# Inverse softmax sums and layer 3 outputs turned by 32x32 blocks on the vector engine and moved by DMA, in a four-layer graph network kernel

## The reference

```python
# layer 0
scores = einsum('bhid,bhjd->bhij', q, k) / sqrt(HD) + edge_bias
attn = softmax(where(adj_mask, scores, -inf), axis=-1)
out = einsum('bhij,bhjd->bhid', attn, v) ...   # then @ W_o.T
# layer 3
e = leaky_relu(e_i[:, :, :, None] + e_j[:, :, None, :], 0.2)
attn = softmax(where(adj > 0, e, -9e15), axis=-1)
out = einsum('bhnm,bhmd->bhnd', attn, h) ...
```

## Time and profile before

| | |
|---|---|
| median of 3 runs | 1429.56 us |
| profiled execution | 1432.08 us, of it the span from first to last instruction 1430.3 us |
| PE busy | 1352.1 us, 95% |
| DVE busy | 1191.3 us, 83% |
| ACT busy | 1188.4 us, 83% |
| POOL busy | 663.1 us, 46% |
| DMA queue of SP | 23618 packets, 44.27 MB, 9.8% of 16 engines' span |
| mean granted TensorE clock | 0.976 |

### The profile page before, as it was taken

One profiled execution on the slowest core, in us unless ns is written; L12 is line 12 of the kernel. 1 busy time (PEld: TensorE's weight loads), 2 busy tenths in 40 slices (PEclk: granted clock), 3 DMA queues, 4 the chain that ended last, 5 costly groups with the idle time before them and its releaser, 6 DMA issues.

```text
span 1430.3 us, 40514 instructions
## 1 busy us (share of the span) xinstructions
PE 1352.1 (95%) x13178; PEld 1075.1 (75%) x13267; DVE 1191.3 (83%) x3407; ACT 1188.4 (83%) x4353; POOL 663.1 (46%) x1014
## 2 busy tenths in 40 slices
PE   4799999999999999999999999999999999999964
PEld 3577788877778887777888777788877778887642
DVE  6568888888888888888888888888888888886763
ACT  3867888889888888998888899888889988887654
POOL 1133445554444555444455544445554444555532
PEclk7899999999999999999999999999999999999986
DMA  3100110011111001111100111111011111100000
GB/s 117 38 31 31 31 31 17 16 39 38 39 38 39 25 16 39 38 38 39 39 29 12 39 39 38 38 39 34 6 39 39 38 39 38 33 8 16 9 15 23
DMA packets 23825, 46.86 MB, mean 33 GB/s; under 512 B 2753, under 2 KB 2754, under 8 KB 23490
## 3 DMA queue, kind: packets, MB, share of 16 engines
q1 hardware_dynamic: 23618, 44.27, 9.8%
HBM read 35.88 MB, written 8.39 MB: 31 GB/s over the span
## 4 chain that ended last, share of the span: by engine, by line
PE 78%; DVE 10%; POOL 5%; issue 4%; ACT 3%; DVEq 0%; POOLq 0%; ACTq 0%
PE B L591 18%; PE B L689 14%; PE B L499 12%; PE B L537 5%; PE B L558 4%; DVE B L1353 4%; DVE x L1326 3%; POOL rstd L376 3%; PE B L808 2%; PE B L523 2%; PE B L788 2%; PE B L754 2%; PE B L581 2%; PE B L665 2%; PE B L683 2%
## 5 line engine op out<-in xcount | busy, mean ns | idle before, releaser
L995 ACT ACTIVATE e<-B,nm 128x128 f32<-128x128 f32 x1024 | 363.9, 385 | 12.5 <-DVE nm L1361 12.0
L499 PEld LDWEIGHTS B<-ident,e 128*128 128x128 f32 x1536 | 187.0, 144 | 104.3 <-issue 75.7
L499 PE MATMUL B<-ident,e 128*128 128x128 f32 x1536 | 230.0, 281 | 9.2 <-ACT e L1151 3.9
L995 ACT ACTIVATION_READ_ACCUMULATOR e<-B,nm 128x1 f32 x1024 | 231.9, 226 | 0.0
L1353 DVE SCALAR_TENSOR_TENSOR B<-an,rowb,mask 128x512 f32<-128x512 f32 x256 | 194.2, 794 | 19.0 <-ACT pT L1004 9.5
L1151 ACT ACTIVATE e<-l,nm 128x128 f32<-128x128 f32 x512 | 198.9, 400 | 10.0 <-DVE nm L1582 9.9
L1361 DVE TENSOR_REDUCE nm<-B 128x4 f32<-128x512 f32 x256 | 166.5, 683 | 35.0 <-PE B L537 34.8
L1004 ACT ACTIVATE pT<-B 128x512 f32<-128x512 f32 x256 | 157.9, 617 | 44.5 <-PE B L499 41.3
L373 POOL TENSOR_TENSOR veps<-meanv,eps 128x4 f32<-128x4 f32 x128 | 41.8, 326 | 328.9 <-DVE meanv L1320 328.8
L376 POOL TENSOR_TENSOR rstd<-veps,neghalf 128x4 f32<-128x4 f32 x128 | 139.7, 1092 | 10.0
L1582 DVE TENSOR_REDUCE nm<-l 128x4 f32<-128x512 f32 x128 | 87.0, 679 | 41.9 <-ACT l L1141 41.9
(11 more groups left out here) (201 smaller groups left out, 3471.1 us busy)
## 6 DMA issues: line engine op xcount, KB each, us to landing
xt<-in_x_t SPq DMA_DIRECT2D x32, 256.0 KB, 3.1
an<-in_adj_n SPq DMA_DIRECT2D x32, 256.0 KB, 2.7
xn<-in_x_n SPq DMA_DIRECT2D x32, 256.0 KB, 3.3
at<-in_adj_t SPq DMA_DIRECT2D x32, 256.0 KB, 3.2
out_x<-xo SPq DMA_DIRECT2D x32, 256.0 KB, 3.5
wm<-in_mats SPq DMA_DIRECT2D x1, 1088.0 KB, 9.4
wm<-in_mats SPq DMA_DIRECT2D x1, 832.0 KB, 7.1
wm<-in_mats SPq DMA_DIRECT2D x1, 320.0 KB, 3.0
```

The costliest lines, as they stand in the source:

```text
L499: last = mm(g(dst, b), g(src, b), ident[:, :], is_transpose=True, start=(b == 0), stop=True, skip_group_check=True)
L995: last = fn(g(e0[:, h % 2, :], b), g(bank, b), ACT.Exp, bias=nm0[:, h % 4, b:b + 1], accum_out=sum0[s % 2][:, b, head(h):head(h) + 1])
```

## The change

Two round trips leave PE and ACT, and the schedule lists of all engines are written anew.

- `spread_sums`, `sums_T` and `keep_sums` are gone. `invert_sums` writes the reciprocals with heads outside. A new `turn_sums` (DVE) transposes the 128 x 32 reciprocals by 32x32 blocks into `recb`. SP writes `recb` to a buffer in HBM with four DMAs of 4 KB (rows of 128 bytes) and reads it back into `recT` with one DMA that repeats each row on 16 partitions.
- `keep_out3` and `out3_T` are gone. A new `turn_out3` (DVE) transposes the 128 x 512 bank by 32x32 blocks into `o3b`. SP writes `o3b` to HBM with one DMA of 256 KB and reads it back into `o3n` with four DMAs of 64 KB, each for 32 partitions, in pieces of 128 bytes, which puts the blocks where a full transpose has them. `divide3` reads `o3n`.
- The five lists are reordered; the banks and the tuples of last users go with them. The program has 41 steps instead of 48.

```diff
-STEPS = GROUPS + 16
+MOVED = 4 * DMA
+STEPS = GROUPS + 9
+            def write_blocks(s, done, sent, got, here, there):
+                wait(sp, q[got], MOVED * s)
+                sp.wait_ge(q[done], s + 1)
+                sp.dma_start(there[:, :], here[:, :]).then_inc(q[sent], DMA)
+            def read_blocks(s, sent, got, there, here):
+                sp.wait_ge(q[sent], DMA * (s + 1))
+                for c in range(4):
+                    sp.dma_start(here[32 * c:32 * c + 32, :].rearrange("r (b i j) -> r b i j", b=GB, i=4),
+                                 there.rearrange("(i r) (b c j) -> c r b i j", i=4, b=GB, c=4)[c]).then_inc(q[got], DMA)
+            def write_sums(s):
+                wait(sp, q["recT_got"], DMA * s)
+                sp.wait_ge(q["rbt_done"], s + 1)
+                for i in range(4):
+                    sp.dma_start(inv_mem.rearrange("h (b i j) -> i (h b) j", b=GB, i=4)[i],
+                                 recb[32 * i:32 * i + 32, :]).then_inc(q["rb_sent"], DMA)
+            def read_sums(s):
+                wait(sp, q["oT_ready"], s)
+                sp.wait_ge(q["rb_sent"], MOVED * (s + 1))
+                sp.dma_start(recT[:, :], inv_mem.unsqueeze(1).broadcast_to([H0, D0, GB * N])).then_inc(q["recT_got"], DMA)
             def step(t):
+                store(t - 8)
                 load_xt(t)
+                write_out3(t - 6)
+                read_out3(t - 6)
+                load_xn(t - 1)
                 load_an(t)
-                load_xn(t)
-                store(t - 8)
                 load_at(t - 1)
+                write_sums(t - 1)
+                read_sums(t - 1)
...
+            def turn_sums(s):
+                wait(dve, q["rb_sent"], MOVED * s)
+                dve.wait_ge(q["rec_done"], s + 1)
+                v.transpose(recb[:, :], rec0[:, :, :].rearrange("p h b -> p (h b)")).then_inc(q["rbt_done"], 1)
...
+            def turn_out3(s, bank):
+                wait(dve, q["o3_sent"], DMA * s)
+                dve.wait_ge(q["pv3_ps"], s + 1)
+                v.transpose(o3b[:, :], bank[:, :]).then_inc(q["o3b_done"], 1)
...
```

More of the change, by code:

```diff
@@ L561, in values @@
                 last.then_inc(q["pv_ps"], 1)
[L563 to L571, removed]
             def project_out(s, bank, users):
@@ L1004, in keep_probs @@
                 fn(pT0[:, h, :], bank[:, :], ACT.Copy).then_inc(q["pT_ready"], 1)
-            def keep_sums(s, bank):
-                if not live(s):
-                    return
-                wait(act, q["oT_ready"], s)
-                act.wait_ge(q["recT_ps"], s + 1)
-                fn(recT[:, :], bank[:, :], ACT.Copy).then_inc(q["recT_ready"], 1)
             def keep_x1(s, bank):
@@ L1655, in step @@
-                norm0(t - 11)
-                half_tanh(t - 12)
-                stats2(t - 13)
-                row_max(t - 10, 7, B[7])
-                aggr2(t - 13)
-                divide3(t - 15, B[4])
-                edge_mask(t - 9)
-                residual3(t - 15)
-                seed_edges(t - 9, 0, B[5], (("pT3_ready", -5, 4, 2), ("pT_ready", -1, 8, 5),
-                    ("exp_done", -1, 8, 5), ("m1_done", -3, 1, 1), ("exp_done", -1, 8, 1)))
-                invert_sums(t - 10)
@@ new lines, in step @@
+                invert_sums(t - 4)
+                shared_to_all(t - 5, B[3])
+                turn_sums(t - 4)
+                message_bias(t - 5, B[4])
+                row_max(t - 3, 0, B[2])
+                row_max(t - 3, 1, B[5])
+                stats3(t - 9)
+                z_times_n(t - 6)
+                row_max(t - 3, 2, B[6])
+                gru_out(t - 6)
+                row_max(t - 3, 3, B[0])
+                sides(t - 5)
+                aggr3(t - 9)
+                shared_to_phases(t - 5, B[3])
@@ new lines, in step @@
+                turn_out3(t - 8, B[2])
+                shared_to_halves(t - 5, B[3], B[2], (("o3b_done", -3, 1, 1), ("exp_done", 2, 8, 1),
+                    ("pT3_ready", -3, 4, 2), ("tz_ready", -1, 1, 1), ("pT_ready", 1, 8, 4),
+                    ("v_ready", 1, 1, 1), ("xc_ready", -1, 1, 1)))
+                stats1(t - 6, B[1])
+                aggr1(t - 6)
+                norm3(t - 9)
+                divide(t - 4, B[7])
+                row_max3(t - 7, 0)
+                seed_edges(t - 3, 4, B[7], (("oT_ready", -1, 1, 1), ("pT_ready", -1, 8, 8),
+                    ("dd_ready", -2, 1, 1), ("qT_ready", 0, 1, 1), ("tr_ready", -3, 1, 1),
+                    ("exp_done", -1, 8, 5)))
@@ new lines, in step @@
+                seed_edges(t - 3, 5, B[5], (("l3_done", -4, 4, 1), ("exp_done", 0, 8, 2),
+                    ("g1_done", -3, 1, 1), ("exp_done", -1, 8, 6)))
+                hidden_bias(t - 6, (B[0], B[6]))
+                norm1(t - 6, B[1])
+                hidden_times_e(t - 6)
+                row_max3(t - 7, 1)
+                seed_edges(t - 3, 6, B[1], (("ln_out1", -3, 1, 1), ("pT_ready", 0, 8, 1),
+                    ("pT3_ready", -5, 4, 3), ("ej_ready", -4, 1, 1), ("pT_ready", -1, 8, 7),
+                    ("x3T_ready", -4, 1, 1), ("exp_done", -1, 8, 7)))
@@ new lines, in step @@
+                seed_edges(t - 3, 7, B[4], (("h3_ready", -4, 1, 1), ("l3_done", -4, 4, 2),
+                    ("pT_ready", 0, 8, 2), ("pT3_ready", -5, 4, 4), ("m1_done", -2, 1, 1),
+                    ("exp_done", -1, 8, 8)))
+                residual0(t - 4, B[6])
+                invert_sums3(t - 8)
+                stats0(t - 4)
+                row_max(t - 3, 4, B[7])
+                row_max(t - 3, 5, B[5])
+                aggr0(t - 4)
+                row_scales(t - 6, (B[3], B[6]))
+                residual2(t - 6, (B[3], B[6]))
@@ L1697, in _ @@
+                stats2(t - 6)
+                aggr2(t - 6)
+                row_max(t - 3, 6, B[1])
+                row_max3(t - 7, 2)
+                divide3(t - 8)
+                residual3(t - 8)
+                edge_mask3(t - 4)
+                norm0(t - 4)
+                row_max(t - 3, 7, B[4])
+                norm2(t - 6)
+                half_tanh(t - 5)
             for t in range(STEPS):
```

497 lines of the change are left out of this document (220 added, 277 removed).

## The result

The changed kernel takes 1433.07 us in the median (1430.38 to 1436.82) against 1430.01 us for the kernel before on the same chip (1428.88 to 1431.28), a ratio of 1.0023 with a 95% interval of 1.0012 to 1.0034. The forecast was 1407 us. The transposes and copies are gone, and the time did not fall.

What follows compares the result with a forecast made beforehand. PE was taken as the bound. From the profiled 1432.1 us, -27.8 for transposes, +1.5 for new idle time and +4 for the ends gave 1409.8; 2.5 less for the median: 1407 us, range 1396 to 1434.

Steps and rivals of the forecast that it cites:

- What bounds the kernel, and what PE loses: PE in the steady part: it sets the step; removed transposes free 0.87 us a group, 27.8 us in all.
- What DVE gets: The two block transposes on DVE: 0.69 and 0.2 us, 0.9 us a step, 37.7 us of work in 40.8.
- What SP gets: SP's list: 5 to 15 issues a step, 0.42 us each, with three new kinds of waits, all hidden or covered.
- (a): Sums' round trip between turn_sums and divide: 6.5 to 7.5 us, hidden behind 12.9 us of DVE instructions.
- (b): Outputs' round trip from turn_out3 to divide3: 12 us (8 to 20), hidden behind 21 us of DVE instructions.
- (c): Loads moved behind SP's new waits: load_an needs 2.7 us before edge_mask, covered by 1.5 us; the others have over 10.
- Rival (2): 128-byte pieces of the outputs' read are slow, divide3 waits past 0.107 us a piece: 1515 us at 0.15; chance 8%.
- The new order: Reordered lists keep PE fed: DVE's step 38.6 us, 0.8 us spare at x1_T; new idle time 0.05 us a step.
- (3): New order loses PE's gain at closest places (x1_T, edge_mask): step near 41.6 us, 1425 to 1433 us; chance 10%.
- (1): DVE becomes the bound, its idle time coming from its list's order: step 42.5 us, 1461 us; chance 8%.
- (4): Ends gain, steps unchanged from forecast: shorter chain saves 20 us, round trip costs 6; 1395 to 1400 us; chance 8%.
- The ends: First and last groups: 10.7 us for the last output, -14 for the shorter list, +3 and +4 at the start: +4.

Runs made afterwards that it cites:

- e9: Kernel before, with GpSimd's three z operations (zplus, zminus, zx) on 16 of 512 columns: 1421.84 us, ratio 0.9943.
- e11: Changed kernel with norm0 ahead of row_max3(2), divide3 and residual3, and GpSimd's three z operations on 16 of 512 columns: 1404.92 us.
- e4: Changed kernel with GpSimd's three z operations (zplus, zminus, zx) on 16 of 512 columns: 1403.54 us, ratio 0.9814 to the kernel before.
- e8: Lists of the kernel before with only the round trip of the layer 3 outputs put in: 1464.58 us, ratio 1.0243.
- e10: Lists of the kernel before with only the outputs' round trip, and GpSimd's three z operations on 16 of 512 columns: 1434.81 us.

## Why the prediction was wrong

**What bounds the kernel, and what PE loses.** PE was the bound of the kernel before, and what leaves it is worth time where it stays fed: right, but less than summed. With PE without a gap in both orders, e9 and e11, the steps differ by 0.64 us, where the distances between starts gave 0.87. The 0.87 us of transposes are gone in full; other products take 0.24 us more in the new list, by the distances between their starts over four steps of e9 and of e11. The rows that show it, first e9, then e11:

```profile
802.33 0.40 PE L659 MATMUL B<-x1T,col 128*32 128x128 f32 x8
802.55 0.40 PE L782 MATMUL B<-x3T,wa 128*32 128x128 f32 x8
```

```profile
828.42 1.06 PE L701 MATMUL B<-wm,x1T 128*128 128x128 f32 x8
829.40 0.43 PE L815 MATMUL B<-x3T,wa 128*32 128x128 f32 x8
829.65 0.40 PE L692 MATMUL B<-x1T,col 128*32 128x128 f32 x8
829.98 1.17 PE L583 MATMUL B<-kh,qT 32*128 32x128 f32 x32
```

`x1T,col` holds PE for 0.22 us, from start to start, in front of a product of its own form (128\*32) and for 0.33 in front of one of another, and `wm,x1T` for 0.98 where it is 0.89 in e9. I had not priced the neighbour here either. That e4's step of 40.67 us meets the 40.7 to 40.9 forecast for a fed PE is partly luck: without collisions a step is 0.32 us shorter in the old order too, and that makes up for the 0.24.

**What DVE gets.** Right for what I priced: 0.716 and 0.194 us against 0.69 and 0.2. The estimate that I had set beside it, from the bf16 figure in "VectorE: DVE Perf Modes" of the Trainium skill, section "The three transpose paths", was 1.24 us for `turn_out3`; the row says 0.716, and decides.

**What SP gets.** Right on the side that mattered, with terms too large. (a) The sums' trip: the step has no wait for it. (b) The outputs: at the end, where nothing hides it, the chain is

```profile
1414.11 0.73 DVE o3b L1600
1414.90 2.00 DMA o_mem<-o3b
...
1418.94 2.35 DMA o3n<-o_mem
1421.41 0.70 DVE r L1608
```

7.3 us with `turn_out3` itself, where I took 12.7. (c) `edge_mask` waits 0.5 us in all. Rival (2), the slow pieces, is out by far: it needed 0.107 us a piece, and a transfer of 512 pieces, 32 for each of the 16 engines, lands in 2.3 us; that makes at most 0.07 us a piece, an estimate from this row.

**The new order.** This step failed: the 0.05 us of new idle time a step, 1.5 us in all. I had laid the durations of before along the new list, got 38.6 us for DVE's step with 2 us in hand and 0.8 us to spare at `x1_T`, and called the order able to keep PE fed. But the durations of before are not the instructions' own: they hold before's collisions with GpSimd, and the new list brings others. `residual3` was 741 ns and became 1029, `edge_mask3` 410 and became 782, the norms from SBUF 415 and became 462, `seed_edges` 794 and became 845: 0.29 + 0.37 + 8 x 0.05 + 8 x 0.05 = 1.4 us a step. `edge_mask` went the other way, 880 to 418, so DVE has only 1.0 us more, but `edge_mask` lies behind `norm0`, outside the loop, and doesn't help `x1_T`. The 0.8 us to spare at `x1_T` became a wait of 0.9. I should have read GpSimd's timeline beside DVE's: the trace of before had the same operation on the same shape at 880 and 410 ns (L1335 and L1343 above), and e9 shows that the neighbour was the reason, for there the 880 are 416.

The steps of e9 (41.31), e11 (40.67), before (41.63) and after (41.68) split this up. Before's step held 0.32 us of collisions with the z work, the transposes were 0.87, the longer products of the new list are 0.24, and the collisions of the new list with the z work 1.01: 41.63 - 0.32 - 0.87 + 0.24 + 1.01 = 41.69 us. So the collisions grew by 0.69 us a step, 21.4 us in all, and the longer products take 31 x 0.24 = 7.4.

**The rivals.** (3) is what happened by its outcome: a step near 41.6, PE idle for 0.84 us where I had written 1.3, 1425 to 1433 us, and the time inside the stated range only because that was drawn wide enough to take this rival in. It named one of the places, `x1_T`; the other, `edge_mask`, held (0.5 us of waits in all), and the collisions, which are the reason, stand nowhere in it. It got 10% since I named the spare 0.8 us and did not ask what could eat it. (1) did not happen: DVE still waits for PE each step (38.2 and 30.1 us). (4) did not happen.

**The ends.** +4 us forecast; 3.1 - 31 x 0.05 = 1.5 measured. The trip at the end added 7.3 - 2.0 = 5.3 us instead of 10.7, and the start's wait of 3.5 us was near the 3 taken; what the shorter list saves there would then be nearer 11 than 14, if the 4 us for `project_out` were right; no run takes the ends apart further.

With the ends at their measured 1.5 us in place of 4, the forecast would have been 1404.5 us. The other 28.6 us up to 1433.07 belong to the new order: the term priced at 1.5 us was 30, of which 21.4 are the new collisions and 7.4 the longer products.

## What to carry to other kernels

When work is moved between engines and the list is reordered, a duration from the old trace is the instruction's own only if nothing ran beside it: for DVE read GpSimd's timeline under it, and price each DVE instruction that reads only SBUF both ways, alone and beside GpSimd. A place with less to spare than one such collision (here 0.3 to 1.0 us) is not covered. On PE, too, a product's price can hang on the form of the one behind it (here 0.1 us). And test the halves of a change apart: here, in the old lists, the sums' half gives 1.2% and the outputs' half takes most of it back.

## What the runs showed of the hardware

- Beside GpSimd's operations on 128x512, DVE instructions on SBUF operands took up to 2.3 times as long in the mean: 706 to 1606 ns for a sum of two 128x512 f32 (e4, e8), 422 to 782 for a one-source 128x512 (e4, after), 663 to 1017 for `divide3` from SBUF (e10, e8). GpSimd's `zminus` suffers too, 639 ns in before against 982. `row_max`, which reads PSUM, did not change: 683 ns before, 681 after, and those of the changed kernel that lie beside a GpSimd instruction take the same 0.68 us. The Trainium skill has this on the page "SBUF — State Buffer", section "Who interferes with whom": only the port pair that DVE and GpSimd share contends, and it is an exclusive lock, so that the one that comes second is blocked wholly. The rows agree: beside GpSimd's one instruction of 1.27 us `norm0` took 1.0 us more.
- DVE doesn't always pay: at 804.82 us of the changed kernel a product of two SBUF tensors (`yT<-zn,zx`) takes its usual 0.68 us, and GpSimd's `ejm` of 804.73 beside it takes 1.01 us, where the mean of one is 0.58. GpSimd's had started first, so which of the two pays doesn't follow from the order of the starts alone.
- Turning 32x32 blocks of f32 on DVE: 716 ns for 128x512 out of PSUM, where the multiply of that width out of PSUM took 691, and 194 for 128x32 from SBUF.
- On TensorE a group of products was 0.1 us longer, by the distance between starts, where the group behind it had another form (128\*128, 128\*32 or 32\*128): 0.33 us against 0.22 and 0.98 against 0.89 (e11, e9).
- Pieces of 128 bytes are cheap here, where they are runs on both sides: 64 KB in 512 pieces land in 2.3 us, a plain 256 KB write in 2.0. The page "VectorE: DVE Perf Modes" of the Trainium skill, section "The three transpose paths", warns of a factor of 19 against the crossbar for a DMA that transposes by its access pattern; on the 2.7 us of a plain load that is an estimate of 51 us. No run here has such a DMA: with the blocks turned on DVE beforehand the four reads took 2.6 us to issue, and each landed in 2.3 us.
